# Expert groups of a patch-embedding, attention and mixture-of-experts block: rows turned two groups ahead, second projection a step later, inner values in two parts

## The reference

```python
h = tok_ref(x, W, b, pos_embed)           # 16 images, 1024 tokens each, 64 channels
h = h + attn_ref(layernorm(h), ...)       # 8 heads of 8 channels, softmax over keys and over a head's channels
h = h + ffn_ref(layernorm(h), gate_w, gate_b, w1, w2, w3)

def ffn_ref(x, gate_w, gate_b, w1, w2, w3):      # 16 experts, hidden 128
    probs = softmax(einsum('bsd,de->bse', x, gate_w) + gate_b)
    top_probs, top_idx = top_k(probs, 2); top_probs /= sum(top_probs)
    h1 = einsum('bsd,edh->bseh', x, w1); h2 = einsum('bsd,edh->bseh', x, w2)
    expert_out = einsum('bseh,eho->bseo', silu(h1) * h2, w3)
    return einsum('bseo,bse->bso', expert_out, dispatch)     # dispatch: the two gates, else 0
```

## Time and profile before

| | |
|---|---|
| median of 3 executions | 1007.12 us (1001.66 to 1008.42) |
| the profiled execution | 997.99 us |
| its span | 996.1 us |
| granted TensorE clock, mean of the span | 0.773 of 2.4 GHz |
| busy: PE, PEld, DVE, ACT, POOL | 684.5, 568.1, 427.0, 339.2, 661.8 us |
| instructions of POOL: indirect DMAs, memsets before them | 512, 512 |

### The profile page before, as it was taken

The page is one execution under the profiler, slowest core; times in us unless marked ns, Lnnn a source line. Parts: engine busy times, 40 slices in busy tenths (PEclk is TensorE's granted clock), DMA queues, the critical chain, the costliest instruction groups (busy, mean ns, idle before and its releaser), DMA issues.

```text
span 996.1 us, 14389 instructions
## 1 busy us (share of the span) xinstructions
PE 684.5 (69%) x3844; PEld 568.1 (57%) x3844; DVE 427.0 (43%) x1045; ACT 339.2 (34%) x657; POOL 661.8 (66%) x1052
## 2 busy tenths in 40 slices
PE   6866676886778677886777777887659556656500
PEld 3555356765775576565755667577657555545400
DVE  4755534642445544453555264534552221112411
ACT  2231112432342444244443354234432332223611
POOL 1050786848588677848884888757884887586085
PEclk9978767877789878878898787977875767657755
DMA  2991312343321732253335243242422333223221
GB/s 62 169 347 75 102 45 85 91 116 101 88 68 43 173 107 74 60 143 91 104 71 118 81 122 90 48 125 80 108 70 70 92 93 80 69 68 78 58 44 31
DMA packets 168871, 93.20 MB, mean 94 GB/s; under 512 B 99680, under 2 KB 152928, under 8 KB 168800
## 3 DMA queue, kind: packets, MB, share of 16 engines
q1 hardware_dynamic: 151632, 66.71, 25.7%
q0 software_dynamic: 16384, 25.20, 9.3%
q10 hardware_dynamic: 784, 0.39, 0.2%
HBM read 45.06 MB, written 47.19 MB: 93 GB/s over the span
## 4 chain that ended last, share of the span: by engine, by line
PE 41%; another core or an unknown queue 25%; issue 12%; DVE 8%; ACT 6%; POOL 4%; DMA 2%; SPq 0%; ACTq 0%; POOLq 0%; DVEq 0%
PE h_ps L1150 11%; PE y_ps L1167 7%; PE hidT_ps L1160 4%; PE wide_ps L1019 4%; PE turn_ps L1135 4%; POOL sums L513 3%; PE wide_ps L1039 2%; ACT sums L633 1%; ACT hidT_all L616 1%; PE wide_ps L1111 1%; PE side_ps L1086 1%; POOL idle L480 1%; DMA rows_all<-rows_scratch 1%; PE wide_ps L1126 1%
## 5 line engine op out<-in xcount | busy, mean ns | idle before, releaser
L495 POOL DMA_INDIRECT rows_scratch<-z_parts,place x256 | 254.4, 994 | 43.6 <-issue 40.7
L480 POOL MEMSET idle<- 128x192 f32 x512 | 140.2, 274 | 196.4 <-issue 62.9
L513 POOL DMA_INDIRECT sums<-y_scratch,place x224 | 219.0, 978 | 36.6 <-issue 33.3
L1150 PE MATMUL h_ps<-w_hi,rowsT 128*128 x384 | 140.7, 382 | 97.6 <-issue 53.7
L1167 PE MATMUL y_ps<-w_sb,hidT_all 128*128 x768 | 128.5, 320 | 94.5 <-issue 49.8
L1167 PEld LDWEIGHTS y_ps<-w_sb,hidT_all 128*128 128x128 f32 x768 | 118.6, 233 | 113.9 <-issue 113.5
L958 DVE SCALAR_TENSOR_TENSOR twice_y<-tanh,h_ps 128x512 f32<-128x512 f32 x96 | 65.9, 686 | 264.2 <-ACT tanh L608 134.7
L1150 PEld LDWEIGHTS h_ps<-w_hi,rowsT 128*128 128x128 f32 x384 | 97.0, 252 | 113.4 <-issue 112.9
L1150 PE MATMUL h_ps<-w_lo,rowsT 128*128 x384 | 129.8, 352 | 0.0
L600 ACT ACTIVATE rowsT<-turn_ps 128x512 fp32r<-128x512 f32 x96 | 57.5, 599 | 183.3 <-remote 112.8
L608 ACT ACTIVATE tanh<-h_ps 128x512 f32<-128x512 f32 x96 | 57.2, 596 | 164.1 <-remote 78.8
(11 more groups left out here) (251 smaller groups left out, 946.3 us busy)
## 6 DMA issues: line engine op xcount, KB each, us to landing
rows_all<-rows_scratch SPq DMA_DIRECT2D x96, 256.0 KB
y_scratch<-twice_y SPq DMA_DIRECT2D x96, 128.0 KB
rows_scratch<-tanh SPq DMA_DIRECT2D x3, 3072.0 KB, 19.4
xi_scratch<-xi SPq DMA_DIRECT2D x16, 256.0 KB
rows_scratch<-z_parts,place POOLq DMA_INDIRECT x256
hx<-xi_scratch SPq DMA_DIRECT2D x14, 256.0 KB
sums<-y_scratch,place POOLq DMA_INDIRECT x224
out<-sums SPq DMA_DIRECT2D x56, 64.0 KB
```

The costliest lines, as they stand in the source:

```text
L480: gp.memset(idle[:, :], 0.0).then_inc(S["idled"], 1)
L495: gp.indirect_dma_start(rows_dram[n], bass.IndirectOffsetOnAxis(ap=place[m % RING][:, r, j:j + 1], axis=0), z_parts[m % 2][:, j // 2, j % ...
L513: gp.indirect_dma_start(y_of[r][apart(m)][:, j // 2, j % 2, :], None, y_dram[m % 3], bass.IndirectOffsetOnAxis(ap=place[m % RING][:, r, j: ...
L1150: mm = te.matmul(h_ps[:, j * 256:(j + 1) * 256], rowsT[g % 2][:, j * P:(j + 1) * P], w[:, bass.ds(e, 1), :, :].rearrange("d a n h -> d (a ...
```

## The change

Each engine's program of a step is written in another order, and one stage is cut in two.

- TensorE turns rows two groups ahead (`turn(g + 2)`), SP loads three ahead, ScalarE copies what TensorE turned in the step before, as the first thing of its step.
- The second projection moves from the end of step g + 1 to step g + 2, right behind `project_in`. ScalarE copies the turned hidden values for it in that step, before the tanh. The copy and the store of y follow a step later.
- `project_in`, the tanh and DVE's two operations work on two halves of a group (`HALVES`, tiles 0 and 1, then 2 and 3), each with semaphore counts of its own, so that `h_done`, `tanh_done`, `twice_done` and `hid_done` count to two per group.
- The gathers of pairs 0, 6 and 7 and the sums of pairs 5, 6 and 7 start a step later, and the loop has 128 steps, not 127.
- The wait of the tanh for the cleared row buffers (`rows_zeroed`) stays.

```diff
-GATHER = (36, 49, 62, 75, 88, 101, 108, 120)
+GATHER = (37, 49, 62, 75, 88, 101, 109, 121)
...
 SP:
-                if 0 <= g + 2 < GROUPS_ALL:
-                    load_rows(g + 2)
-                if 0 <= g - 2 < GROUPS_ALL:
-                    store_y(g - 2)
+                if 0 <= g + 3 < GROUPS_ALL:
+                    load_rows(g + 3)
+                if 0 <= g - 3 < GROUPS_ALL:
+                    store_y(g - 3)
 POOL:
-                    wait(pool, "rowsT_ps_ready", s - LAG + 1)
+                    wait(pool, "rowsT_ps_ready", min(s - LAG + 2, GROUPS_ALL))
 ACT:
             def activate(g):
-                wait(act, "h_done", g + 1)
-                wait(act, "twice_done", g)
...
-                sc.activation(tanh[:, :, :], h_ps[:, :].rearrange("p (j n h) -> p j n h", j=GROUP, n=2)[:, :, 0, :],
-                              ACT.Tanh, scale=0.5).then_inc(S["tanh_done"], 1)
+                for i, j in enumerate(HALVES):
+                    wait(act, "h_done", 2 * g + i + 1)
+                    wait(act, "twice_done", 2 * g + i - 1)
+                    sc.activation(tanh[:, j, :], h_ps[:, :].rearrange("p (j n h) -> p j n h", j=GROUP, n=2)[:, j, 0, :],
+                                  ACT.Tanh, scale=0.5).then_inc(S["tanh_done"], 1)
...
+                if 0 <= g + 1 < GROUPS_ALL:
+                    turn(g + 1)
+                if 0 <= g - 3 < GROUPS_ALL:
+                    copy_y(g - 3)
+                if 0 <= g - 2 < GROUPS_ALL:
+                    copy_hidT(g - 2)
                 for m, k in steps_at(s):
                     attend(m, k)
-                if 0 <= g - 2 < GROUPS_ALL:
-                    copy_y(g - 2)
                 if 0 <= g < GROUPS_ALL:
                     activate(g)
-                if 0 <= g - 1 < GROUPS_ALL:
-                    copy_hidT(g - 1)
-                if 0 <= g + 1 < GROUPS_ALL:
-                    turn(g + 1)
 DVE, multiply(g):
-                ve.scalar_tensor_tensor(twice[:, :, :], tanh[:, :, :], 1.0, halves[:, :, 0, :], ALU.add, ALU.mult).then_inc(S["twice_done"], 1)
-                wait(dve, "twice_done", g + 1)
                 wait(dve, "hidT_ps_ready", g - 1)
-                ve.scalar_tensor_tensor(hid[g % 2][:, :, :], twice[:, :, :], 0.5, halves[:, :, 1, :], ALU.mult, ALU.mult).then_inc(S["hid_done"], 1)
+                for i, j in enumerate(HALVES):
+                    wait(dve, "tanh_done", 2 * g + i + 1)
+                    wait(dve, "hid_done", 2 * g + i - 1)
+                    ve.scalar_tensor_tensor(twice[:, j, :], tanh[:, j, :], 1.0, halves[:, j, 0, :], ALU.add, ALU.mult).then_inc(S["twice_done"], 1)
+                    wait(dve, "twice_done", 2 * g + i + 1)
+                    ve.scalar_tensor_tensor(hid[g % 2][:, j, :], twice[:, j, :], 0.5, halves[:, j, 1, :], ALU.mult, ALU.mult).then_inc(S["hid_done"], 1)
 PE, project_in(g):
-                wait(pe, "hid_done", g)
-                for j, e in enumerate(experts[g]):
+                for i, half in enumerate(HALVES):
+                    wait(pe, "hid_done", 2 * g + i - 1)
+                    for j in range(half.start, half.stop):
...
+                    mm.then_inc(S["h_done"], 1)
...
                 if 0 <= g < GROUPS_ALL:
                     project_in(g)
+                if 0 <= g - 2 < GROUPS_ALL:
+                    project_out(g - 2)
                 if 0 <= g - 1 < GROUPS_ALL:
                     turn_hidden(g - 1)
                 for m, k in steps_at(s):
                     attend(m, k)
-                if 0 <= g + 1 < GROUPS_ALL:
-                    turn(g + 1)
+                if 0 <= g + 2 < GROUPS_ALL:
+                    turn(g + 2)
                 for m, k in steps_at(s):
                     attend(m, k + 0.5)
-                if 0 <= g - 1 < GROUPS_ALL:
-                    project_out(g - 1)
```

More of the change, by code:

```diff
@@ L947, in find_owners @@
                 if m >= 3:
-                    wait(dve, "h_done", GROUPS * (m - 2))
+                    wait(dve, "h_done", 2 * GROUPS * (m - 2))
                 ve.tensor_scalar(owner[m % 3][:, :], sides[second(m)][0:1, 258:258 + TILES], float(EXPERTS - 1), None,
@@ L1146, in project_in @@
                 wait(pe, "rowsT_ready", g + 1)
[L1147 to L1152 removed]
+                for i, half in enumerate(HALVES):
+                    wait(pe, "hid_done", 2 * g + i - 1)
+                    for j in range(half.start, half.stop):
+                        for w, first in ((w_hi, True), (w_lo, False)):
+                            mm = te.matmul(h_ps[:, j * 256:(j + 1) * 256], rowsT[g % 2][:, j * P:(j + 1) * P],
+                                           w[:, bass.ds(experts[g][j], 1), :, :].rearrange("d a n h -> d (a n h)"), start=first, stop=not first)
+                    mm.then_inc(S["h_done"], 1)
             def turn_hidden(g):
[L1155 removed]
+                wait(pe, "hid_done", 2 * g + 2)
                 wait(pe, "hidT_ready", g)
```

12 lines of the change are left out of this document (3 added, 9 removed).

## The result

The changed kernel took 1045.15 us (median of 4, 1043.54 to 1047.42), the kernel before on the same chip 1004.39 us (median of 4, 1001.23 to 1008.42): 1.0405 of the time before, 95% interval 1.0353 to 1.0458, 41 us slower. The prediction was 961 us, and its range ended at 1030.

The account below looks back on a forecast made before the run. No engine was full: TensorE waited for signals late while GpSimd streamed, GpSimd for TensorE's steps. Shorter steps save 54 us, the start costs 7, so 1007 - 47 = 960, with one more for instructions 961 us; range 915 to 1030.

Parts of the forecast that it names:

- Second projection a step later: TensorE's second projection waiting for ScalarE: 94.4 us of waits would shrink but not vanish.
- Both ends: all 94.4 us go, or none: Bounds on the saving at the second projection's waits for ScalarE: between all 94.4 us and nothing.
- A signal up to 1.4 us late costs nothing: At the second projection, lateness up to 1.4 us would be covered; a signal 6 us late would still cost 4.6.
- Rows turned two groups ahead: At project_in: its 39.6 us in 17 waits for ScalarE's copy of turned rows would go.
- The halves: Tanh and VectorE work cut in two: extra instructions run beside TensorE's work; nothing counted for the shorter chain to hid.
- The start: First turn ahead of pair 1's count: first group at 165.4 us, +7 us, bounds 0 and +10.
- The later gathers and sums: Gathers and sums a step later, and the 128th step: 0 us.
- The sum: Average step from 8.17 to 7.6 us over 95 steps: 54 us saved, with the start's 7 us set against it.
- The floors: Least time per step: 7.5 us for TensorE in the middle, 7.4 us for GpSimd where it streams beside late pairs.
- Late signals add up: Rival: 96 more TensorE signals, each possibly held for a GpSimd DMA period, 99 us in all; 1059 us, chance 0.21.
- The wait only moves: Rival: the second projection waits as long behind ScalarE's copy of the rows; 994 or 998 to 1012 us, chance 0.14.
- PE comes clear of POOL: Rival: GpSimd's waits for steps go except one per pair, a step of 7.0 us; 903 us, chance 0.11.

Follow-up runs that it names:

- the edit that takes the long step away: Changed kernel with TensorE running gate logits and patch embedding ahead of the second projection in eight steps: 864.03 us, 1.0210 of the kernel before.

## Why the prediction was wrong

**"Second projection a step later" is the step that failed.** It set a chain of 1.6 us (copies of rows, y and hidden values) against a cover of 3 us. The chain is longer, and it starts later: ahead of the three copies ScalarE has what its .5 stages left over, z_parts with 2.1 us or values and exponentials of the queries with 1.4 us and a wait for VectorE, and these in turn need what TensorE does last in its step. In the long step the copy of the hidden values began 2.6 us after `project_in` (370.9 to 373.53) and took 0.6. The step also counted no one behind the waiting projection, where turned hidden values, logits, embedding and the next turn stand. Before, the projection was last and nothing of its own step stood behind it. The waits went to 177.5 us instead of below 50 (to 71.6 where signals are on time). "Both ends: all 94.4 us go, or none" left out that they can grow.

**"A signal up to 1.4 us late costs nothing" had a second fault.** The price of a wait is not its length where the clock falls behind it: 2.09 us became 6.8. (That TensorE's work takes about half the time at 2.4 GHz is right, but not by the 0.28 and 0.40 us that the prediction names; the logits show it, 1.87 and 3.46 us.)

**"Rows turned two groups ahead" was right in the wait, and wrong in its worth.** The wait for copied rows went, in the changed kernel and with this part alone. Alone it made steps 0.08 us shorter, 8 us in all, and the time 0.998 of before. Where signals are on time it gives nothing beside the late projection (1.0011 with both, 0.998 and 0.999 with the projection alone).

**The halves.** Counted at nothing; 7 us alone where signals are late (interval 1.0022 to 1.0119), none where they are on time (1.0108 beside 1.0109). Since the interval begins near 1, how much of it is the additional signals is not settled.

**The start.** Forecast 7 us, first group at 165.4; measured 167.7, and 6 to 8 us in the time where it could be priced. The later gathers and sums cost nothing, as said (0.998 in the version with the projection g-2 at the end, which has the same shift).

**The sum** put a step at the higher of two floors, 7.6 us. It came to 8.53, and GpSimd's waits for steps, which were to fall from 127 to 75 us, rose to 46.7 + 117.2 + 25.5 = 189. The floors themselves were too high. Where signals are on time, the changed kernel's steps take (801.3 - 167.1) / 95 = 6.68 us on average and those with the projection g-2 at the end (750.8 - 156.9) / 95 = 6.25 us:

```profile
L1157 PE MATMUL h_ps<-w_hi,rowsT x384: 276/287/578, 167.1 to 801.3; 128*128 x192
...
L1150 PE MATMUL h_ps<-w_hi,rowsT x384: 276/292/578, 156.9 to 750.8; 128*128 x192
```

The 7.5 us for TensorE were its busy time at the granted clock of the earlier trace rows, 0.82, which is no constant: in the second of these kernels it is 0.92 to 0.94 through the middle. The 7.4 us for GpSimd counted 64 DMAs to every pair's steps, while in the same trace only 418 of the 512 start between the first and the last `project_in`: 418 x 1.39 / 95 = 6.1 us.

**The rivals.** "Late signals add up" gave 1059 us and is nearest in time, but that is luck: its mechanism is refuted twice, by the kernel without the halves (1.0425) and by the changed kernel where no signal is late (1.0507). "The wait only moves" had the right queue, ScalarE's copies in order, and stopped at no change; the wait grew. "PE comes clear of POOL" did not occur, and its premise, a denser TensorE, was turned round. Of the signs that the prediction named, the last one decided: a new wait of the second projection on the copy, longer than the old.

What stays open: where signals are late, the five long steps alone make some 49 us, and the last 25 groups then take 15 us less than before; that the sum is about that of the other chips (41 and 43.5 us) may be chance, and the edit that takes the long step away was measured only where signals are on time. And the version with the projection g-2 at the end was not measured where signals are late, where TensorE and not GpSimd sets the step.

## What to carry to other kernels

A step that is moved earlier in an in-order queue is paid for by everything behind it, so its cover must be counted against the whole queue of the engine that feeds it, from that engine's leftovers of the step before to the copy, in the step with the most small work and not in the average one. Where a pipeline stage gets a step of slack, take it as slack (same place, older group), and leave the place at the end of the step; where signals are on time, the version made so had 8 us of waits at the second projection and the changed one 72. It then cost nothing here, but it gained nothing either. And put a wait behind TensorE's dense stretch, not ahead of it.

## What the runs showed of the hardware

The kernel before took 995 to 1004 us in three measurements and 844 to 847 us in three others, on other chips (medians; single runs 988 to 1015 and 842 to 852). What differs in the traces is that updates of TensorE's semaphores reach their waiters late on the first kind while GpSimd streams indirect DMAs, all ten traces having waits of the kind remote, and never on the second, where none of ten traces has one and GpSimd streams at the same 1.39 us per DMA. So GpSimd is the bound on the second kind and not on the first. A chip did not change its kind while it was measured; but all measurements of the first kind came before those of the second, so what sets it, the chip, the hour or something beside the kernel, no run here shows. What the prediction took for a property of the hardware did not hold for every chip.

The other surprise is the price of a short wait: TensorE was busy 2.19 of 4.3 us around a wait of 2.09 us, at a granted clock of 1.00, and the next 10.7 us had 0.52 of 2.4 GHz, the 1.2 GHz level for nearly all of them.
